# A masked 3x3 convolution after channel attention: its taps moved to four 64x64 quarters of the systolic array

## The reference

```python
MASK[:, :, K // 2, K // 2:] = 0.0      # of the middle row only the left tap stays
MASK[:, :, K // 2 + 1:] = 0.0          # nothing of the row below
wt = wt.reshape(b * DIM, 1, K, K) * jnp.tile(MASK, (b, 1, 1, 1))
out = jax.lax.conv_general_dilated(x.reshape(1, b * c, h, w), wt, window_strides=(1, 1), padding=((1, 1), (1, 1)), feature_group_count=b * DIM, ...)
```

## Time and profile before

| | |
|---|---|
| median of 3 runs | 215.45 us (215.25 to 218.28) |
| span of the profiled execution | 216.9 us |
| TensorE, VectorE, GpSimd, ScalarE busy | 96%, 88%, 80%, 62% |
| DMA | 79.18 MB, mean 365 GB/s |

### The profile page before, as it was taken

The page is one execution under the profiler, slowest core; times in us unless marked ns, Lnnn a source line. Parts: engine busy times, 40 slices in busy tenths (PEclk is TensorE's granted clock), DMA queues, the critical chain, the costliest instruction groups (busy, mean ns, idle before and its releaser), DMA issues.

```text
span 216.9 us, 2648 instructions
## 1 busy us (share of the span) xinstructions
PE 207.2 (96%) x814; PEld 126.3 (58%) x814; DVE 190.0 (88%) x224; ACT 135.3 (62%) x208; POOL 172.9 (80%) x168
## 2 busy tenths in 40 slices
PE   7999989999999999999999999999999999999990
PEld 3458564475666566656655764675556656665550
DVE  4238679887999999999999999999999999889991
ACT  2020015568585768576857687677657796989960
POOL 0222049999999999999999999999999996887880
PEclk9999976999999999999999999999999999999997
DMA  5999999859999999999999999999999475627777
GB/s 154 360 424 429 431 422 427 372 178 326 386 417 390 400 420 421 424 435 423 423 435 428 426 419 430 428 426 431 423 426 396 192 298 222 262 111 296 296 304 290
DMA packets 8526, 79.18 MB, mean 365 GB/s; under 512 B 1056, under 2 KB 1440, under 8 KB 2496
## 3 DMA queue, kind: packets, MB, share of 16 engines
q1 hardware_dynamic: 8352, 78.91, 88.4%
q10 hardware_dynamic: 160, 0.10, 0.2%
HBM read 40.48 MB, written 38.54 MB: 364 GB/s over the span
## 4 chain that ended last, share of the span: by engine, by line
PE 54%; DVE 27%; DMA 9%; ACT 3%; SPq 3%; issue 2%; ACTq 0%; DVEq 0%
PE banks L913 43%; DVE banks L668 12%; DMA xin<-x 9%; DVE xout L668 5%; DVE xout L677 4%; PE banks L898 2%; ACT banks L748 2%; PE banks L842 2%; PE banks L905 2%; PE banks L884 2%; PE banks L886 2%; DVE stats L556 1%; DVE sums L575 1%; SPq L363 1%; DVE stats L572 1%
## 5 line engine op out<-in xcount | busy, mean ns | idle before, releaser
L913 PE MATMUL banks<-xin,diag 128*128 128x495 f32 (+4 forms) x480 | 159.1, 483 | 0.3 <-ACT banks L748 0.2
L913 PEld LDWEIGHTS banks<-xin,diag 128*128 128x128 f32 x480 | 88.5, 191 | 54.7 <-issue 39.0
L748 ACT ACTIVATE banks<-xin,wide_sb,coef 128x616 f32<-128x616 f32 (+5 forms) x77 | 84.8, 1120 | 20.1 <-DVE xout L677 9.4
L417 POOL TENSOR_TENSOR halves<-xin 128x1568 f32<-128x1568 f32 (+1 forms) x22 | 73.7, 3348 | 20.1 <-DMA xin<-x 20.0
L668 DVE SCALAR_TENSOR_TENSOR banks<-xin,coef,banks 128x1485 f32<-128x1485 f32 (+2 forms) x48 | 82.0, 1707 | 2.2 <-ACT banks L748 1.2
L668 DVE SCALAR_TENSOR_TENSOR xout<-xin,coef,banks 128x1485 f32<-128x1485 f32 (+5 forms) x31 | 41.6, 1362 | 0.6
L422 POOL TENSOR_TENSOR halves<-halves 128x784 f32<-128x784 f32 x18 | 33.3, 1850 | 1.4
L677 DVE SCALAR_TENSOR_TENSOR xout<-xin,coef,banks 128x990 f32<-128x990 f32 (+2 forms) x24 | 29.2, 1215 | 4.0 <-PE banks L913 3.8
L744 ACT ACTIVATE diag<-wide_sb,coef 128x128 f32<-128x128 f32 x72 | 23.4, 389 | 6.7 <-DVE coef L602 6.7
L789 ACT ACTIVATE xout<-banks 128x616 f32<-128x616 f32 (+3 forms) x24 | 16.0, 667 | 15.8 <-PE banks L913 15.3
L427 POOL TENSOR_TENSOR rows<-halves 128x392 f32<-128x392 f32 x18 | 18.3, 1019 | 1.4
(11 more groups left out here) (83 smaller groups left out, 133.9 us busy)
## 6 DMA issues: line engine op xcount, KB each, us to landing
xin<-x SPq DMA_DIRECT2D x23, 1568.0 KB, 10.3
out<-xout SPq DMA_DIRECT2D x23, 1568.0 KB, 12.5
xout<-x SPq DMA_DIRECT2D x3, 392.0 KB, 4.5
xin<-x SPq DMA_DIRECT2D x1, 1120.0 KB, 15.6
out<-xout SPq DMA_DIRECT2D x1, 616.0 KB, 3.3
out<-xout SPq DMA_DIRECT2D x1, 476.0 KB, 3.9
xin<-x SPq DMA_DIRECT2D x1, 448.0 KB, 16.2
wide_sb<-wide SPq DMA_DIRECT2D x1, 435.5 KB, 16.6
```

Source lines behind the costliest of these rows:

```text
L417: eng.tensor_tensor(halves[:, j % 2, first:end, :], cells[:, :, 0, :], cells[:, :, 1, :], ALU.add).then_inc(once_folded, 1)
L748: return sca.activation(acc, above_rows(k, first, end), ACT.Identity, bias=bias[:, k % PER:k % PER + 1], scale=weight(k, UP))
L913: return mm(to, diag[:, k % 2, which, :], grid(k)[:, irows, cols], start=False, stop=(which == LEFT), skip_group_check=True)
```

## The change

A diagonal matrix uses only two of the four 64 x 64 quarters of the array. After the change a tap is two products with 64 x 64 diagonals. On the straight quarters (partitions 0 to 63 to 0 to 63, and 64 to 127 to 64 to 127) they serve 27 rows (`b_rows`, three chunks of 9): ScalarE seeds, TensorE adds two taps, VectorE the last. On the crossed quarters (0 to 63 to 64 to 127, and back) they serve 14 rows (`s_rows`, two chunks of 7): TensorE does all four taps, ScalarE copies them out with the bias; they then lie in the other half of the partitions, and two stores of 64 partitions each bring them to their place. VectorE has 15 rows of its own. `fold_thrice` goes, and VectorE sums 784 elements where it summed 392. The rows of the last six tiles on GpSimd and ScalarE go, and so do the splits of the first and last tiles. A diagonal is 64 columns wide, and there are four a tile for three.

```diff
-FIRST_ROWS = (22, 18, 16, 0)
-ROWS = (27, 18, 11, 0)
-TAIL_ROWS = (24, 16, 9, 7)
-LAST_ROWS = (22, 17, 10, 7)
-AHEAD_FOLD = 6
-BANK_A, BANK_B, BANK_D, BANK_S = 0, 2, 4, 7
+D_ROWS = 15
+B_ROWS = 9
+B_CHUNKS = 3
+S_ROWS = 7
+S_CHUNKS = 2
+TOP_B = D_ROWS
+TOP_S = TOP_B + B_CHUNKS * B_ROWS
+BANK_G, BANK_B, BANK_D, BANK_S = 0, 2, 5, 7
+HALF = P // 2
+STORES = 3
+HALVES = (slice(0, HALF), slice(HALF, P))
...
+            def store_crossed(k, first, end):
+
+                for own, other in (HALVES, HALVES[::-1]):
+                    sp.dma_start(out_tiles[k // PER, k % PER][own, first * W:end * W],
+                                 xout[other, k % OUT_BUFS, first * W:end * W]).then_inc(stored[k % OUT_BUFS], 16)
...
-                sp.wait_ge(b_out, k + 1)
+                sp.wait_ge(conv_s, S_CHUNKS * (k + 1))
+                sp.wait_ge(b_out, B_CHUNKS * (k + 1))
                 sp.wait_ge(edge_out, k + 1)
                 if k + IN_BUFS < TILES:
                     load(k + IN_BUFS).then_inc(loaded[k % IN_BUFS], 16)
                 sp.wait_ge(d_out, k + 1)
-                sp.wait_ge(a_out, k + 1)
-                if tail(k):
-                    sp.wait_ge(part_out, k + 1 - (TILES - AHEAD_FOLD))
-                store(k)
+                sp.wait_ge(s_out, S_CHUNKS * (k + 1))
+                store(k, 0, TOP_S)
+                store_crossed(k, TOP_S, H)
...
                 if k > 0:
-                    finish_mixed(k - 1)
-                tap(k, LEFT_UP, 0, top_b(k)).then_inc(tap0_done, 1)
+                    finish_b(k - 1, 2)
+                if t == 2 and ahead:
+                    gained_step(g + 1)
+                tap(k, LEFT_UP).then_inc(tap0_done, 1)
                 if k == 0:
                     sum_ahead(AHEAD - 1)
+                finish_b(k, 0)
+                if t == 2 and ahead:
+                    coef_steps(g + 1)
+                tap(k, RIGHT_UP).then_inc(tap2_done, 1)
...
+                finish_b(k, 1)
+                tap(k, LEFT).then_inc(d_out, 1)
...
             for k in range(TILES):
                 g, t = k // PER, k % PER
-                seed_b(k)
+                if k > 0:
+                    finish_s(k - 1, 1)
+                seed_b(k, 2)
                 if t == 1 and g + 1 < NGROUP:
                     lift_relu(g + 1)
-                if tail(k):
-                    part(k)
-                finish_array(k)
+                finish_s(k, 0)
                 if t == 1 and g + 1 < NGROUP:
                     hidden_relu(g + 1)
                 if k + 1 < TILES:
-                    diagonals(k + 1)
-                    seed_a(k + 1)
+                    for which in (LEFT_UP, UP, RIGHT_UP, LEFT):
+                        diagonal(k + 1, which)
+                    seed_b(k + 1, 0)
+                    seed_b(k + 1, 1)
                     seed_d(k + 1)
...
+            def add_b(k, c, which):
+
+                irows, cols, ocols = window(*b_rows(c), which)
+                to = acc_b(c).rearrange("p (r c) -> p r c", c=W)[:, :, ocols]
+                for own in HALVES:
+                    ins = mm(to[own], diag[own, k % 2, which, :], grid(k)[own, irows, cols],
+                             start=False, stop=(which == RIGHT_UP), skip_group_check=True)
                 return ins
 
+            def add_s(k, c, which):
+
+                irows, cols, ocols = window(*s_rows(c), which)
+                to = acc_s(c).rearrange("p (r c) -> p r c", c=W)[:, :, ocols]
+                for own, other in (HALVES, HALVES[::-1]):
+                    ins = mm(to[other], diag[own, k % 2, which, :], grid(k)[own, irows, cols],
+                             start=(which == UP), stop=(which == LEFT), skip_group_check=True)
                 return ins
...
+                pe.wait_ge(diag_done, TAPS * k + (2 if k == 0 else TAPS))
+                begin_b(k, 0)
+                begin_s(k, 0)
+                add_s(k, 0, LEFT_UP)
+                if k == 0:
+                    pe.wait_ge(diag_done, TAPS)
+                end_b(k, 0)
+                add_s(k, 0, RIGHT_UP)
                 if t == 1 and ahead:
                     mix(g + 1)
...
                 if t == 2 and ahead:
                     spread_taps(g + 1)
-                mixed_taps(k, 0)
+                begin_b(k, 1)
+                end_s(k, 0)
+                end_b(k, 1)
+                begin_s(k, 1)
+                add_s(k, 1, LEFT_UP)
+                begin_b(k, 2)
+                add_s(k, 1, RIGHT_UP)
                 if t == 1 and ahead:
                     hide(g + 1)
-                mixed_taps(k, 1).then_inc(conv_b, 1)
+                end_b(k, 2)
+                end_s(k, 1)
                 if t == 1 and ahead:
                     make_taps(g + 1)
```

More of the change, by code:

```diff
@@ L95, with b_rows, s_rows @@
 S_END = S_ABOVE + C
[L98 to L123, removed]
+def b_rows(c):
+    return TOP_B + c * B_ROWS, TOP_B + (c + 1) * B_ROWS
+def s_rows(c):
+    return TOP_S + c * S_ROWS, TOP_S + (c + 1) * S_ROWS
 def build(nc, x, early, narrow, wide, out):
@@ L276, in window @@
                 return rows, slice(1, W), slice(0, W - 1)
+            if which == UP:
+                return rows, slice(0, W), slice(0, W)
             return rows, slice(0, W - 1), slice(1, W)
@@ L436, in _ @@
                 fold_once(j)
-            def part_rows(k):
-                n = k - (TILES - AHEAD_FOLD)
-                top, rows = top_p(k), H - top_p(k)
-                scaled = part_scaled_of(k)
-                own = part_own(k)
-                for product, which in enumerate((RIGHT_UP, LEFT)):
-                    irows, cols, ocols = window(top, H, which)
-                    each = weight(k, which).rearrange("p (r c) -> p r c", r=1).broadcast_to([P, rows, W - 1])
-                    eng.tensor_tensor(own[product], grid(k)[:, irows, cols], each, ALU.mult).then_inc(part_product, 1)
-                pool.wait_ge(part_seeded, n + 1)
-                pool.wait_ge(part_product, 2 * n + 1)
-                to = result(k)[:, top:H, 0:W - 1]
-                eng.tensor_tensor(to, to, own[0], ALU.add).then_inc(part_step, 1)
-                to = result(k)[:, top:H, 1:W]
-                pool.wait_ge(part_product, 2 * n + 2)
-                pool.wait_ge(part_step, 2 * n + 1)
-                eng.tensor_tensor(to, to, own[1], ALU.add).then_inc(part_step, 1)
-                pool.wait_ge(part_scaled, n + 1)
-                pool.wait_ge(part_step, 2 * n + 2)
-                eng.tensor_tensor(to, to, scaled, ALU.add).then_inc(part_out, 1)
             for k in range(TILES):
@@ L651, in _, with tap @@
             dve.wait_ge(pad_zeroed, 1)
-            vec.tensor_scalar(acc_d(0, 0, top_b(0)), above_rows(0, 0, top_b(0)), weight(0, UP), bias[:, 0:1],
+            vec.tensor_scalar(acc_d(), above_rows(0, 0, D_ROWS), weight(0, UP), bias[:, 0:1],
                               ALU.mult, ALU.add).then_inc(seeded_d, 1)
-            def tap(k, which, first, end):
-                irows, cols, ocols = window(first, end, which)
+            def tap(k, which):
+                irows, cols, ocols = window(0, D_ROWS, which)
                 if which == LEFT_UP:
@@ L739, in hidden_relu, with diagonal @@
                                scale=a_hid[:, :]).then_inc(hidden_done, 1)
-            def diagonals(k):
+            def diagonal(k, which):
                 act.wait_ge(coef_done, k // PER + 1)
-                for which in (LEFT_UP, RIGHT_UP, LEFT):
-                    sca.activation(diag[:, k % 2, which, :], ident, ACT.Copy, scale=weight(k, which)).then_inc(diag_done, 1)
+                sca.activation(diag[:, k % 2, which, :], eye, ACT.Copy, scale=weight(k, which)).then_inc(diag_done, 1)
             def seed(k, acc, first, end):
@@ L749, in seed, with seed_b @@
                                       scale=weight(k, UP))
-            def seed_a(k):
+            def seed_b(k, c):
                 if k > 0:
-                    act.wait_ge(a_out, k)
-                seed(k, acc_a(k), top_a(k), top_p(k)).then_inc(seeded_a, 1)
-            def seed_b(k):
-                if k == 0:
-                    act.wait_ge(warmed, 1)
-                else:
-                    act.wait_ge(b_out, k)
-                seed(k, acc_b(k), top_b(k), top_a(k)).then_inc(seeded_b, 1)
@@ L834, in prime @@
             def prime(bank):
-                for b in range(bank, bank + 2):
-                    mm(banks[:, b, :], zeros[:, 0:P], zeros[:, :], start=True, stop=True)
+                mm(banks[:, bank, :], zeros[:, 0:P], zeros[:, :], start=True, stop=True)
             def keep_warm(products, columns=BANK):
                 for _ in range(products):
-                    ins = mm(banks[:, BANK_B + 1, 0:columns], zeros[:, 0:P], zeros[:, 0:columns], start=True, stop=True)
-                return ins
+                    mm(banks[:, BANK_G + 1, 0:columns], zeros[:, 0:P], zeros[:, 0:columns], start=True, stop=True)
             prime(BANK_B)
+            prime(BANK_B + 1)
             warm(1)
```

(1 more changed line is left out.)

201 lines of the change are left out of this document (75 added, 126 removed).

## The result

The changed kernel takes 218.83 us (median of 3 runs, 218.15 to 220.18) where the one before takes 215.45: the ratio is 1.013, with an interval of 1.007 to 1.020. The forecast was 202. (The profiled executions of two experiments, 222.31 and 221.72 us, were disturbed ones, some 5 us above their medians; what is read from them is shown for those executions only.)

A forecast was written before the change was run, and what follows sets the result against it. TensorE and VectorE were both taken as full, with the DMA full beside them. First tile at 43 us, 18 tiles at 6.9, 5 at 6.1, plus 4.4 us to the end give 202 us; range 191 to 325 us.

The forecast's parts named there:

- Queue and DMA: Loads and stores: one load and three stores a tile on SP; compute at 6.9 us just avoids the DMA's pace.
- the price of the crossed rows: Stores of 14 of 56 rows in 3,136-byte runs: at 374 GB/s, 3 us more DMA, 0.13 us a tile.
- just fits: Middle tiles: four output buffers give a store 20.7 us; landing needs 12.1 + 8.4 = 20.5 us by tile 14.
- SP's queue: Issuing of loads and stores: a store holds SP 0.42 us, so 0.83 us more of a 6.9 us tile.
- the last stores are as small as before: End of kernel: from VectorE's last step to the end of the span stays 4.4 us.
- TensorE's quarters: TensorE's taps: four quarters stream side by side, 5.2 us a tile; without any overlap 20.3 us.
- Two at a time: Rival, TensorE's taps: program order lets only neighbouring calls half overlap, 10.17 us a tile, 308 to 345 us; chance 0.38.
- No change: Rival, whole tile: quarters overlap, but lockstep or the DMA keeps a tile at 7.3 us, 215 us; chance 0.1.
- Shape changes: TensorE around the four small products: 8 array-shape changes a group cost 0.24 to 1.3 us a tile, taken as 0.3.
- the prediction's own subtraction: Weight-load idle at a shape change: 0.73 less 0.23 between taps less 0.415 tap stream leaves 0.09 us lost.
- VectorE's steps by shape: VectorE per tile: taps 1.067, finishing steps 0.727, sum 0.96 us; 6.75 us, with waits pacing at 6.9.
- ScalarE: ScalarE's seeds, copies and diagonals: 6.0 us a tile, covered, but limiting the last five tiles to some 6.1 us.

The follow-up runs named there:

- two experiments: Kernel before with the change's three stores, halves straight: 217.14 us, ratio 1.001; and changed kernel with five output buffers instead of four: 216.85 us, ratio 1.001.
- the two runs without halves: Changed kernel with one 128-partition store a tile: 205.73 us; and with two stores of all partitions, rows 0 to 41 and 42 to 55: 207.31 us.
- one store: Changed kernel, each tile but the last leaving in one store of 128 partitions and 56 rows: 205.73 us, ratio 0.951.
- few rows out: Changed kernel storing only VectorE's first 15 rows of each tile but the last, in one DMA, 41 rows left out: 202.05 us.
- even and odd partitions: Changed kernel, its two 64-partition stores taking even and odd partitions instead of lower and upper half, rows written straight: 208.33 us, ratio 0.960.
- all rows in halves: Changed kernel with two straight stores a tile, each of 64 partitions and all 56 rows: 213.13 us, ratio 0.982.

## Why the prediction failed, step by step

**The step that failed** is "Queue and DMA", and in it the price of the crossed rows, "3 us more of DMA, 0.13 us a tile". A tile's 3.2 MB takes 7.5 us at 427 GB/s and 8.1 us at the 396 GB/s measured: 0.6 us a tile, taken over all its traffic. I priced the length of the runs, by the first stage at 374 GB/s, and no term asked which partitions a store reads; the two runs without halves put the run length at 3 to 4 GB/s. By an estimate with 0.6 instead of 0.13, compute at 6.83 us gains 1.3 us a tile on the DMA, so the slack of 8.4 us that "just fits" is gone after some 6 tiles of lag, not 14; measured, the first late tile is the tenth after the first. The prediction had the condition right ("the middle thus just doesn't fall back to the DMA's pace") and nothing in hand. The same step mis-sized SP's queue as well: it took 0.42 us for each further store, 0.83 us a tile, and a half store holds SP for 1.36 us, 2.7 us a tile. What that costs by itself is not shown.

In numbers, against the forecast span end of 202.1 us: first tile 42.6 for 43 (-0.4); nine tiles 61.5 for 62.1 us (-0.6); the ten late ones 83.2 for 9 x 6.9 + 6.1 = 68.2 (+15.0); the last four 24.1 for 24.4 (-0.3); from VectorE's last step to the end 6.8 for 4.4 (+2.4). Together 218.2. The same ten tiles take 69.8 us with one store and 66.7 with few rows out. So of the 15, 13.4 are the stores' form, 3.1 the DMA at its full rate, and compute took 1.5 back by beating the forecast's 68.2. "Just fits" was thus nearly right at 425 GB/s: with one store, tiles are late only from the sixteenth after the first on. The +2.4 is a small step that failed as well: "the last stores are as small as before" forgot that the last tile's end now has half stores in it. SP's last two lines (start, length) show it: VectorE's last step ends at 211.4 us, and the last store is issued 2.9 us later, behind two half stores that hold SP for 1.86 us.

```profile
212.44 1.86 SPq L335 DMA_DIRECT2D out<-xout  x2
214.35 0.98 SPq L329 DMA_DIRECT2D out<-xout  x1
```

**TensorE's quarters** did what the forecast took. The timeline of the changed kernel (start, length, engine, line; x is the instructions merged):

```profile
95.62 0.63 PE L833 MATMUL banks<-xin,diag 64*64 64x495 f32 x2
95.64 0.87 PE L842 MATMUL banks<-xin,diag 64*64 64x392 f32 x4
96.06 0.61 PE L833 MATMUL banks<-xin,diag 64*64 64x495 f32 x2
96.34 0.49 PE L842 MATMUL banks<-xin,diag 64*64 64x385 f32 x2
96.47 0.61 PE L833 MATMUL banks<-xin,diag 64*64 64x495 f32 x2
96.67 0.49 PE L842 MATMUL banks<-xin,diag 64*64 64x385 f32 x2
96.89 0.61 PE L833 MATMUL banks<-xin,diag 64*64 64x495 f32 x2
...
100.84 0.63 PE L833 MATMUL banks<-xin,diag 64*64 64x495 f32 x2
```

The straight pair starts at 95.62, the crossed pair 0.02 us later: four quarters are in flight. The straight ones follow at 0.42 us (95.62, 96.06, 96.47, 96.89), the crossed ones at 0.33 us (96.34, 96.67), each at the pace that its columns had before. From this tile's first tap to the next tile's, from 95.62 to 100.84 us, it is 5.2 us as forecast.

**The rival "Two at a time"** is refuted by the same rows. The four crossed products merged at 95.64 are the two instructions of a call on two quarters; in the trace's single records the second ones start at 96.01 us, ahead of the straight call's second ones at 96.06, which stand earlier in the program. The Trainium skill (TensorE: Matmul & The Clock Gate, Part 3: Packing small matmuls) has products start and end strictly in program order; here, with float32 products of two instructions on separate quarters, the trace differs in the starts, and 5.2 us a tile instead of 10.17 decides.

**The rival "No change"** (215 us) came nearest, by the branch that it names second: the DMA. It was near by luck, since its price was a constant 7.3 us a tile; measured are 6.83 us for nine tiles and 8.3 for ten.

**Shape changes and VectorE.** The weight load path of the changed kernel idles 0.60 us ahead of L824, one of the four small stages:

```profile
90.63 0.14 PEld L842 LDWEIGHTS banks<-xin,diag 64*64 64x64 f32 x2 [0.18 <-issue]
91.37 0.74 PEld L824 LDWEIGHTS banks<-taps,wide_sb 96*128 96x128 f32 x6 [0.60 <-issue]
```

Between two taps the path idles 0.18 us. By the prediction's own subtraction, with a tap's stream of 0.33 or 0.42 us, 0.60 - 0.18 leaves 0.09 us or nothing, which is the lower bound or less, and it doesn't show in the sum. VectorE's steps by shape, as forecast from the earlier trace rows: 0.724 us for 0.727, 1.076 for 1.067, and the interpolated sum 0.960 for 0.96.

```profile
L616 DVE SCALAR_TENSOR_TENSOR xout<-xin,coef,banks 128x495 f32<-128x495 f32 x72 | 52.1, 724 | 19.4 <-DMA out<-xout 15.5 <-PE banks L833 3.9
L606 DVE SCALAR_TENSOR_TENSOR banks<-xin,coef,banks 128x825 f32<-128x825 f32 x48 | 51.7, 1076 | 10.0 <-ACT banks L684 10.0
...
L494 DVE TENSOR_REDUCE stats<-halves 128x49 f32<-128x784 f32 x18 | 17.3, 960 | 0.0
```

Of the 19.4 us that it stood idle ahead of its finishing steps, 15.5 were behind stores.

**ScalarE** was put at 6.1 us as the limit of the last tiles; they take 5.4, so that bound was too high by 0.7 us.

**What the halves do.** The Trainium skill (SBUF — State Buffer, Door 1: The DMA port swizzle) says that DMA reaches the partitions through 16 ports, that partitions 0 to 63 lie behind eight of them and 64 to 127 behind the other eight; by its table the even partitions lie behind all 16. The order of the runs agrees: halves 396 to 416 GB/s, even and odd partitions 421, all of them 422 to 425. Its size agrees only in part: an estimate from that page, with crossed bytes at half of 425 GB/s, is 2.8 MB/425 + 0.4 MB/212 = 8.5 us a tile (8.1 measured), but 11.3 us with all rows in halves, where 416 GB/s, 7.7 us, were measured. The single packets in the traces (65 to 165 us) show another picture than a halved rate. A packet of 3,136 bytes takes 124 ns in the median in the changed kernel, and the same with even and odd partitions; but the mean is 150 ns against 126, because 12% of the packets take over 1.3 times the median, against 0.2%. The 9,408-byte packets of the long store beside them go from 357 to 384 ns in the mean, the loads' of 12,544 bytes only from 476 to 481. So most packets run at their usual pace and some stall, in the half stores and in the stores beside them. That halves lower the rate is shown; by which of ports, order on the rings or engines is not, and why long halves cost less than short ones stays open. A single store of all 128 partitions that puts crossed rows in their place was not tried.

## What to carry to other kernels

When a change splits a transfer, ask which partitions each piece touches as well as its bytes and run length: here that was the larger price. Give a piece partitions from both halves, or (not tried here) compute so that nothing crosses. Where the DMA is full beside compute, work out at which tile the buffers' slack runs out for a rate a tenth lower as well: if "just fits" decides the forecast, its range must hold the other case with a large chance. Judge a DMA change in a kernel that is fast enough to feel it; the slower kernel's time did not move with three stores a tile.

## What the hardware showed beyond that

TensorE's clock fell where the DMA starved it. The stages of the changed kernel around one such place:

```profile
172.00:176.00 4.00, 1.61 (x18) 0.65 (x10) 2.25 (x3) 2.20 (x6) 3.30 (x5) 1.00 0.98 346
176.00:178.00 2.00, 1.92 (x18) 1.19 (x20) 1.97 (x3) 1.65 (x2) 0.00 (x0) 0.79 0.79 260
178.00:180.00 2.00, 2.00 (x12) 0.85 (x6) 1.93 (x5) 0.99 (x3) 0.88 (x3) 0.50 0.57 175
...
182.00:184.00 2.00, 2.00 (x18) 1.29 (x14) 0.33 (x2) 0.59 (x1) 0.68 (x3) 0.50 1.00 355
184.00:186.00 2.00, 2.00 (x26) 0.70 (x18) 1.52 (x2) 0.44 (x2) 0.20 (x1) 1.00 0.75 215
```

TensorE is busy for only 1.61 of 4 us while it waits for a late tile, and after it has begun again the granted clock drops from 1.00 (2.4 GHz) to 0.50 (1.2 GHz) until about 184 us. A wait of 2.5 us is so followed by some 7 us at half speed, a second price of a late store that no term of the sum had.

The rate of 396 GB/s stands at a DMA share of 1.01, the same as 425. The share counts the time in which engines have a packet in hand, and stalled packets fill it too; only the GB/s beside it told the two kernels apart.
